# Vector quantisation behind group norm: low halves made by TensorE and ScalarE, and ScalarE sums the products of all sixteen tiles

## The reference, cut to what matters

```python
x = x + _L0_conv_ref(_gn(x), weights1, weights2)
x = x + _L1_conv_ref(_gn(x), embeddings)
```

```python
flat = x.reshape(-1, D)
distances = y_sq + e_sq - 2.0 * jnp.einsum('nd,dk->nk', flat, embeddings)
codes = jnp.argmin(distances, axis=1)
quantized = jnp.take(embeddings.T, codes, axis=0)
```

## Time and profile before

| | |
|---|---|
| median of 3 runs | 7373.56 us (7361.45 to 7394.95) |
| profiled execution, its own time | 7382.31 us |
| its span | 7380.5 us |
| TensorE busy | 6392.3 us (87%) |
| VectorE busy | 6776.5 us (92%) |
| ScalarE busy | 4352.2 us (59%) |
| GpSimd busy | 5114.3 us (69%) |
| mean granted TensorE clock | 0.887 |

### The profile page before, as it was taken

The page is one execution under the profiler, slowest core; times in us unless marked ns, Lnnn a source line. Parts: engine busy times, 40 slices in busy tenths (PEclk is TensorE's granted clock), DMA queues, the critical chain, the costliest instruction groups (busy, mean ns, idle before and its releaser), DMA issues. The chain is left out here.

```text
span 7380.5 us, 130164 instructions
## 1 busy us (share of the span) xinstructions
PE 6392.3 (87%) x24080; PEld 2436.6 (33%) x24080; DVE 6776.5 (92%) x18796; ACT 4352.2 (59%) x11681; POOL 5114.3 (69%) x4614
## 2 busy tenths in 40 slices
PE   7998788888888888888888888888898888888887
PEld 3458233333223333333333333333333333333232
DVE  7771699999999999999999999999999999999998
ACT  2331566656666666666666666666666666666665
POOL 0000577777877777777777777777777777777777
PEclk9998889888998888888988888988888888889987
DMA  7979455555555555555555555555555555555554
GB/s 253 307 252 186 97 143 137 132 130 135 134 142 132 137 135 134 135 141 136 134 134 138 138 136 134 134 140 135 137 132 134 135 137 137 137 135 136 139 135 106
DMA packets 1110238, 1073.54 MB, mean 145 GB/s; under 512 B 690656, under 2 KB 830752, under 8 KB 1109472
## 3 DMA queue, kind: packets, MB, share of 16 engines
q1 hardware_dynamic: 895968, 651.56, 33.0%
q0 software_dynamic: 196608, 411.30, 25.0%
q10 hardware_dynamic: 16896, 4.20, 0.3%
HBM read 722.32 MB, written 143.01 MB: 117 GB/s over the span
## 5 line engine op out<-in xcount | busy, mean ns | idle before, releaser
L980 POOL DMA_INDIRECT arena<-table,idx x4096 | 4237.7, 1035 | 1451.9 <-issue 1215.2
L673 ACT ACTIVATE arena<-bank 128x512 f32<-128x512 f32 x4096 | 2432.3, 596 | 2421.3 <-PE bank L515 2340.1
L515 PE MATMUL bank<-eh,t 128*128 128x512 f16 x8192 | 2764.6, 422 | 830.9 <-DVE mx L872 605.2
L872 DVE CUSTOM_DVE_ANT_0 arena<-bank,arena 128x512 f32<-128x512 f32 x4096 | 2771.4, 677 | 160.3 <-ACT arena L673 108.3
L882 DVE FIND_INDEX8 idx<-mx,arena 128x8 uint32<-128x512 f32 x4096 | 2811.0, 686 | 0.0
L515 PE MATMUL bank<-el,t 67*128 67x512 f16 x8192 | 2747.7, 420 | 0.0
L515 PEld LDWEIGHTS bank<-eh,t 128*128 128x128 f16 x8192 | 629.7, 105 | 2851.4 <-ACT arena L673 1766.8
L515 PEld LDWEIGHTS bank<-el,t 67*128 67x128 f16 x8192 | 873.7, 107 | 1186.6 <-issue 377.1
L987 POOL TENSOR_TENSOR X<-X,arena 128x1024 f32<-128x1024 f32 x256 | 606.2, 2368 | 13.7 <-DVE arena L909 7.8
L494 PE MATMUL conv<-X,ident 128*128 128x512 f32 x1024 | 598.1, 668 | 5.8 <-ACT Ts L610 5.8
L499 PE MATMUL conv<-iw,Ts 64*128 64x512 f32 x1024 | 599.2, 666 | 0.0
(11 more groups left out here) (102 smaller groups left out, 3915.6 us busy)
## 6 DMA issues: line engine op xcount, KB each, us to landing
X<-x SPq DMA_DIRECT2D x512, 512.0 KB, 4.5
y<-X SPq DMA_DIRECT2D x256, 512.0 KB, 3.0
t<-t SPq DMA_DIRECT2D x256, 256.0 KB
arena<-table,idx POOLq DMA_INDIRECT x4096
arena<-w SPq DMA_DIRECT2D x12, 2048.0 KB, 22.8
arena<-w SPq DMA_DIRECT2D x64, 128.0 KB, 3.0
spec<-Fs SPq DMA_DIRECT2D x256, 16.0 KB, 3.5
Xc<-spec SPq DMA_DIRECT2D x16, 256.0 KB, 8.6
```

Source lines behind the costliest of these rows:

```text
L515: last = nc.tensor.matmul(bank[4 + k % 2 if e else k % 4][:], tile[0:rows, g.buf2, k], codes[0:rows, e], start=rows == P, stop=rows != P)
L673: nc.scalar.activation(R[:, k % 4], bank[4 + k % 2][:], ACT.Relu).then_inc(b_rl, 1)
L872: V.tensor_tensor_reduce(out=Fm[:, k % 4], in0=bank[k % 4][:], in1=R[:, k % 4], scale=1.0, scalar=-3.0e38, op0=ALU.add, op1=ALU.max, accum ...
L980: G.indirect_dma_start(out=q[:, g.buf2, k], out_offset=None, in_=table, in_offset=bass.IndirectOffsetOnAxis(ap=idx[:, g.buf2, k, 0:1], axis=0)
```

## The change

- **Low halves.** `low_half` leaves VectorE. TensorE makes it in `conv`: identity by Y in float32, then minus identity (`nid16`, new) by YS in fp16, for each of the two banks, behind the scores of tiles 5 and 6. ScalarE copies it to YS (`take_low`) behind the relu of tile 7.
- **Sums.** `sum_products` leaves VectorE. ScalarE sums the products of all sixteen tiles: three behind each relu of tiles 9 to 12, four behind tile 13.
- **Banks.** Bank 3 becomes `aux`, for `inverse_h` and `statistics`. The even scores run round three banks instead of four. The count runs over the eight groups of a loop turn, so `scores(n)` waits for `best(n-3)`; at the first three tiles of a turn for n-2, n-2 and n-5.
- **Places.** `add_x` and `inverse_w` move from tiles 4 to 7 to tiles 10 to 13, `inverse_h` from 15 to 14. `take_x` moves from tile 9 to 14. `square_sum`, `statistics`, `delta2_of`, `variance_of` and the deviation move to tiles 1, 4, 5, slot 11 and 7 of the next group; `scale_of` and `bias_of` from 8 to 13, behind the four sums; `high_half` from tile 0 to tile 15 of the group before.

```diff
+            def low_half(g, t, taken):
+                if t == 0:
+                    need(pe, b_y, g.n + 1)
+                    need(pe, b_x1, taken)
...
+                ks = slice(t * (NT // T2), (t + 1) * (NT // T2))
+                cv = conv[:, t].rearrange("p (k d) -> p k d", d=D)
+                nc.tensor.matmul(cv, ident[:], Y[:, g.buf4, ks], start=True, stop=False)
+                nc.tensor.matmul(cv, nid16[:], YS[:, ks, 0:D], start=False, stop=True).then_inc(b_low, 1)
...
+            return bank[(NT * (g.r % U) + k) % 3]
+            return {0: 2, 1: 2, 2: 5}.get(NT * (g.r % U) + k, 3)
...
-                need(pe, b_ttr, n - 3)
+                need(pe, b_ttr, n - score_lag(g, k) + 1)
...
                     for k in range(NT):
                         scores(g, k)
+                        if two.exists() and k == 4:
+                            statistics(two)
+                        if one.exists():
+                            if k == 5:
+                                low_half(one, 0, two.n + 1 if two.exists() else NG)
+                            if k == 6:
+                                low_half(one, 1, NG)
                         if three.exists():
-                            if k == 4:
+                            if k == 10:
                                 add_x(three, 0)
-                            if k == 5:
+                            if k == 11:
                                 inverse_w(three, 0)
-                            if k == 6:
+                            if k == 12:
                                 add_x(three, 1)
-                            if k == 7:
+                            if k == 13:
                                 inverse_w(three, 1)
-                            if k == 14:
-                                statistics(three)
...
+            def take_low(g):
+                need(act, b_low, T2 * (g.n + 1))
+                nc.scalar.copy(YS[:, :, D:2 * D], conv[:].rearrange("p t (k d) -> p (t k) d", d=D)).then_inc(b_yl, 1)
...
                         relu(g, k)
-                        if before.exists() and k in (10, 12, 13, 14):
-                            for n in range(2):
-                                sum_product(before, NT - TA + 2 * (10, 12, 13, 14).index(k) + n)
+                        if before.exists() and 9 <= k < 14:
+                            for n in range(3 * (k - 9), NT if k == 13 else 3 * (k - 8)):
+                                sum_product(before, n)
...
-            def low_half(g):
-                need(dve, b_y, g.n + 1)
-                hold(dve, "dve", g.n)
-                V.tensor_tensor(YS[:, :, D:2 * D], Y[:, g.buf4], YS[:, :, 0:D], ALU.subtract).then_inc(b_yl, 1)
...
-            def sum_products(g):
-                need(dve, b_p, g.n + 1)
-                V.tensor_reduce(dot[:, 0:NT - TA], prod[:, 0:NT - TA], AX_X, ALU.add).then_inc(b_red, 1)
```

More of the change, by code:

```diff
@@ L58 @@
 ROW = 3 * D + 4
-TA = 8
 DC = float((2 * (H - 1)) * (2 * (W - 1)))
@@ L514, in scores @@
                     for e in range(2):
-                        last = nc.tensor.matmul(bank[4 + k % 2 if e else k % 4][:], tile[0:rows, g.buf2, k],
+                        last = nc.tensor.matmul(bank[4 + k % 2][:] if e else score_bank(g, k)[:],
+                                                tile[0:rows, g.buf2, k],
                                                 codes[0:rows, e], start=rows == P, stop=rows != P)
@@ L708, in _ @@
                 delta2_of(Group(0, r))
-                if r < 2:
-                    scale_of(Group(0, r))
-                    bias_of(Group(0, r))
                 if r == 0:
+                    scale_of(Group(0, 0))
+                    bias_of(Group(0, 0))
                     high_half(Group(0, 0))
                     normalise(Group(0, 0))
+            take_t(Group(0, 2))
+            take_x(Group(0, 2))
+            scale_of(Group(0, 1))
+            bias_of(Group(0, 1))
+            high_half(Group(0, 1))
             body_b(0)
@@ L718, in _ @@
             body_b(NI - 1)
-            for k in range(NT - TA, NT):
+            for k in range(NT):
                 sum_product(Group(NI - 1, U - 1), k)
@@ L871, in best @@
                 hold(dve, "dve", g.n)
-                V.tensor_tensor_reduce(out=Fm[:, k % 4], in0=bank[k % 4][:], in1=R[:, k % 4], scale=1.0,
+                V.tensor_tensor_reduce(out=Fm[:, k % 4], in0=score_bank(g, k)[:], in1=R[:, k % 4], scale=1.0,
                                        scalar=-3.0e38, op0=ALU.add, op1=ALU.max,
@@ L912, in small_step @@
             def small_step(g, k, at):
-                before, one, three = (Group(g.i, g.r + n) for n in (-1, 1, 3))
+                before, two = Group(g.i, g.r - 1), Group(g.i, g.r + 2)
                 slot = 2 * k + at
@@ L919, in small_step @@
                         products(before)
-                    if slot == 14:
-                        sum_products(before)
                     if slot == 29:
@@ L925, in small_step @@
                         settle(before)
-                if one.exists() and slot == 7:
-                    low_half(one)
-                if three.exists():
-                    if slot == 31:
-                        variance_of(three)
+                if two.exists():
+                    if slot == 11:
+                        variance_of(two)
             def body_b(i):
@@ L942, in body_b @@
                         small_step(g, k, 1)
-            for r in range(3):
+            for r in range(2):
                 variance_of(Group(0, r))
-                if r == 0:
-                    low_half(Group(0, 0))
             body_b(0)
@@ L955, in _ @@
             products(last)
-            sum_products(last)
             choose(last)
@@ L991, in body_b @@
                     g, before = Group(i, r), Group(i, r - 1)
-                    three = Group(i, r + 3)
+                    two = Group(i, r + 2)
                     for k in range(NT):
@@ L996, in body_b @@
                             finish(before)
-                        if three.exists() and k == 15:
-                            inverse_deviation(three)
+                        if two.exists() and k == 7:
+                            inverse_deviation(two)
             pool.wait_ge(tab_out, 16)
```

94 lines of the change are left out of this document (57 added, 37 removed).

## The result

The changed kernel takes 7848.92 us, median of 4 runs (7830.78 to 7864.07). The kernel before took 7367.51 us in the same comparison. The ratio is 1.0651, with a 95% interval of 1.0605 to 1.0697: it is 6.5% slower. The forecast was slower by 3.6%, 7640 us, and the range reached to 7980; the measured time lies at the very end of the forecast's inner range (7480 to 7850). The profiled execution has a span of 7828.9 us, 448.4 more than before.

A forecast was written before the change was run, and what follows sets the result against it. VectorE was taken as the bound, with a gathered-rows chain almost as long. 9.5 (part one) + 16.1 (part two) + 1.0 on top = 26.6 us a group, 1.0 over 25.60, times 256: 7640 us, range 7270 to 7980.

The forecast's parts named there:

- What bounds the kernel: VectorE, busy 92%, and a second chain through the gathered rows almost as long, with 73.0 us of waits.
- Part one: From the end of find(14) to the start of products: 9.67 us in the group read, forecast 9.5.
- the gain is 0.24: Between find(14) and products: removing low_half gains 0.24 us, not 1.13, because the gathered rows come after 9.67.
- Part two at full clock: From products to the end of the next find(14): forecast 16.1 us, against 15.29 in the group read.
- What comes on top: Addition per group for half-clock stretches and loop turns: 1.0 us in all instead of 0.64.
- The first rival: Long half-clock stretches over tiles 10 to 15, about 8075 us if in every second group; chance 0.18 (7850 to 8200).
- The backlog of work: Argument against long half-clock stretches: queued TensorE work closes the idle place, so clock falls can't follow in each group.
- A sign that was wrong: Over the whole run: a mean clock well below 0.85 would show that long half-clock stretches had come.
- TensorE and ScalarE keep up: Rival at tile 14's relu: no lateness there, part two 14.70, group 24.8, about 7190 us; chance 0.20.
- The floor named there: GpSimd, from one gather of tile 14 to the next: 24.85 us, taken as about the lowest group time.
- VectorE's work alone: Rival: all 1.13 + 0.59 = 1.72 us taken off VectorE come through, 6940 us; chance 0.03.
- The port rule: Two-input VectorE operations and GpSimd operations reading SBUF block one another; without low_half GpSimd's floor sinks a little.

The follow-up runs named there:

- e10: Kernel before with low_half cut to one number of 64, the rest of that work left out: 7292.76 us, ratio 0.9916.
- e1: Changed kernel with six filler fp16 matmuls behind scores(9), in TensorE's idle place: 7431.89 us, ratio 1.0081.
- e2: Changed kernel with add_x and inverse_w at tiles 9, 9, 11, 12 instead of 10 to 13: 7348.96 us, ratio 0.9966.
- e5: e2 with ScalarE's sums 5, 4, 3, 2, 2 behind tiles 9 to 13, scale and bias behind 12: 7267.76 us, ratio 0.9899.
- e3: Kernel before with its even scores in three banks instead of four: ratio 1.003 from eight of ten executions.
- e7: Changed kernel with GpSimd's gather of tile 15 issued ahead of finish, nothing else: 7184.84 us, ratio 0.9774.
- e4: Kernel before with all sixteen sums on ScalarE at the changed kernel's places, none on VectorE: 7365.0 us, ratio 1.0008.
- e8: Kernel before with GpSimd's gather of tile 15 issued ahead of finish, nothing else: 7434.09 us, ratio 1.0117.
- e11: e10 with GpSimd's gather of tile 15 issued ahead of finish as well: 7251.12 us, ratio 0.986.

## Why the prediction was right and where it was wrong

**What bounds the kernel: right.** There are two chains through part one, and the one through the gathered rows was nearly as long as VectorE's. e10 shows it alone: 1.0 us of VectorE's work removed brought 0.32 a group.

**Part one: the number right, in part by luck.** Forecast 9.5, measured 9.44 (median) with waits of 256.4 us where 280 was forecast. VectorE's own path would be 8.28, forecast 8.43. But the prediction set out from one group with 9.67, and that was a short one: over groups 8 to 244 of the kernel before, part one is 10.04 in the median and 10.30 on average. So the change took 0.6 off it, where 0.17 was forecast.

Most of that is the landing. Where `products` waits for it, `products` starts 4.59 behind the end of the last gather's issue before (median of 124 groups; 4.57 in e10, where the transpose is still in it), and 4.11 after (211 groups). So the landing is 0.48 shorter, where 0.17 was taken for the transpose; the short group and the small term made up for one another. That it was the transpose alone, no run shows. And that "the gain is 0.24" does not follow from the rows: 0.24 is VectorE's wait in that group, and by the chain read there the removal of `low_half` alone gains nothing. The low halves took TensorE 1.08 us for each bank; that cost nothing that a wait shows, and neither did the move of the transpose on SyncE.

**Part two at full clock: right.** Forecast 16.1, measured 16.17 in the 46 groups that had full clock there and in nearly all groups of e1. Here the group read was typical: 15.29, with a median of 15.23 and a mean of 15.38 before. `best(14)` was forecast at 12.05 and came at 12.11; `best(15)` at 13.55 and 13.60. Both reasons stand: TensorE's heavy tiles (e2: 15.71 once they are moved) and ScalarE's burst (e5: 14.73 once that is spread too, where 14.70 was VectorE's wish).

**"What comes on top": the step that failed.** The prediction took 1.0 us a group for half clock and loop; measured are 27.35 - 25.6 = 1.75. This is the term that was mis-sized, and all of the miss: 0.75 x 256 = 192 us, and 7638 + 192 = 7830 is the profiled execution. The term was worked out as a share of a group in four that pays for one tile's store. What the trace shows instead is a fall in three groups of four (178 of 237) at the idle place ahead of scores(10), and each short stretch costs 1.67 us because it lies on `add_x` and scores(11), the path itself. The thirteen long stretches, some 8.1 us each, add the rest. By groups: 1.67 x 178 / 237 + 8.1 x 13 / 237 = 1.70. The 0.64 of the kernel before, from which the term set out, lay elsewhere, in part one: 11.45 on average in the first group of each loop turn, 10.43 in the other groups with half clock in part one (100), 9.86 in those without (107). What the change moved is where half clock falls, from there and the light tiles to the heavy ones.

**The first rival had the mechanism.** The idle time of TensorE ahead of its heavy work makes the clock fall over tiles 10 on. It had the shape wrong: not long stretches in every second group but short ones in most. The backlog of work that spoke against it did not keep the falls away; whether it is what keeps most of them short, no run shows. The rule named there (the Trainium skill, TensorE: Matmul & The Clock Gate, "A second HAM failure mode: psum-queue depth-cycling", on short idle times in PSUM cycling) agrees in kind with the trace, though the depth of the ring by itself cost no more than 0.6% in the eight executions of e3.

**A sign that was wrong.** The prediction would have taken a mean clock well below 0.85 as the rival's mark. The mean clock rose, from 0.887 to 0.919, while the time rose by 6.5%. Between 1000 and 7200 us the trace has 1396 us of half clock before and 990 after. But before, what lay in part two fell on light tiles and cost little: part two is 15.22 in the median, and 15.58 on average even in the 71 groups with over 7 us of half clock in it. After, less of it lies where nothing covers it.

**The other rivals.** TensorE and ScalarE keep up: didn't come. e5 makes it true in the typical group, with a part two of 14.73, but takes 7268 us where 7190 was worked out. e7, at 7185, is not this rival: its part two is 16.15, and the time comes from part one and the clock. The floor named there, 24.85 us from one gather of tile 14 to the next, is none of GpSimd's: in the kernel before that gather starts 0.81 behind `find(14)` in nearly all groups, so these rows tell how often VectorE reaches it. VectorE's work alone: e4 and e10 each show why not. The port rule, which the prediction set beside this rival, was the one that changed most later on: in e8 and e11 a VectorE step with two SBUF inputs waited for the end of GpSimd's add, as the Trainium skill (SBUF — State Buffer, "Who interferes with whom", on the shared port pair) says. In the kernel before `low_half` and `finish` overlap in no group.

**What stays open.** Why the clock falls at the idle place in three groups of four and not in all. The 46 groups without a fall there are no random ones: 29 are the first of a loop turn, and 9 of the others had half clock in part one already; the last 8 stay unexplained. Versions with less GpSimd work were not tried, nor was the full removal of `low_half` by itself.

**What the loop costs.** e7's mean group ((7167.9 - 842.5) / 255 = 24.81, from the starts of its first and last `choose`) is 0.4 us longer than its typical one. It is the loop's turn: part one is 11.28 on average in the first group of each turn and 8.21 in the other 207, and 3.07 / 8 = 0.38.

```profile
L947 DVE TENSOR_TENSOR odd<-dot,arena x256: 155/167/186, 842.5 to 7167.9; 128x16 int32<-128x16 f32 x128
```

## What to carry to other kernels

Before an engine is relieved, find the second chain that ends beside it: removed work is worth the slack to that chain and no more, and here one gather behind one add was that chain. Don't put TensorE's heaviest work right behind its idle place: here it then ran at half clock, on the path. Ask where the half-clock stretch lies, not what the mean clock is. One group read in full is not yet the typical group: take the median over all of them before a sum is built on it. A change that loses may still lie on the way to one that wins: the changed kernel is 6.5% slower, the earlier gather alone 1.2% slower (e8), and both together are 2.3% faster (e7).

## What the runs showed of the hardware that was not expected

- Six fp16 matmuls of no use, 1.46 us, in front of a 0.75 us wait, gave back 417 us of 7849: the granted clock went from 0.92 to 0.99 (from 2000 to 7000 us).
- A VectorE step of 16 numbers per partition, two SBUF inputs, took 1258 ns instead of 214 when GpSimd's add of 2.36 us was under way, and `low_half` (1024 numbers) 1909 instead of 1207.
- An indirect gather is 0.95 us of GpSimd and starts 1.25 us behind the one before. Beside `COPY_PREDICATED` of VectorE one took 2.01 (e7, 4002.95, with `COPY_PREDICATED` from 4002.88 to 4004.18). Of the gathers that start during one, 231 of 237 take over 1.2 us in the changed kernel and 66 of 254 in e7 (why so few there is open); of those that started ahead of one, none does:

```profile
4001.58 0.95 POOL L1016 DMA_INDIRECT arena<-table,idx  x1 [0.31 <-issue]
4002.95 2.01 POOL L1016 DMA_INDIRECT arena<-table,idx  x1 [0.42 <-issue]
```
